# Two output tiles of chunk 14 multiplied while its y are made, the other four one behind the other, chunk 15's products in a new order

## What is computed

```
hs  = groupnorm(x)                        # per pixel 768 channels, 4096 pixels an image
xs  = silu(depthwise_conv3x3(hs @ in_proj.T) + conv_b)      # 1536 channels
dt, B, C = split(xs @ x_proj.T)           # 48, 4 and 4 columns
delta = softplus(dt @ dt_w + dt_b)
h[t] = exp(delta*A) * h[t-1] + (delta*xs)*B       # a scan over the pixels, 4 states a channel
y   = sum_n h[t,n]*C[t,n] + D*xs
y   = layernorm over the 1536 channels
x   = x + y @ out_proj.T                  # 768 channels
```

## Time and profile before

| | |
|---|---|
| time, median of 3 runs | 3519.16 us (3517.67 to 3519.83) |
| the profiled execution's own time | 3515.45 us |
| its span, first to last instruction | 3513.4 us |
| TensorE busy / VectorE / ScalarE / GpSimd | 3303.4 / 2848.3 / 2436.5 / 2366.1 us |
| mean granted TensorE clock | 0.980 |
| layer 0's last addition to x, end | 2601.5 us |
| layer 1's first instructions | 2604.0 us |

### The profile page before, as it was taken

The page is one execution under the profiler, slowest core; times in us unless marked ns, Lnnn a source line. Parts: engine busy times, 40 slices in busy tenths (PEclk is TensorE's granted clock), DMA queues, the critical chain, the costliest instruction groups (busy, mean ns, idle before and its releaser), DMA issues. The chain is left out here.

```text
span 3513.4 us, 38815 instructions
## 1 busy us (share of the span) xinstructions
PE 3303.4 (94%) x10616; PEld 1690.2 (48%) x10616; DVE 2848.3 (81%) x4084; ACT 2436.5 (69%) x4194; POOL 2366.1 (67%) x1566
## 2 busy tenths in 40 slices
PE   5967999999999999999999999997989999999998
PEld 2422343434334343443433434342347877777887
DVE  7799999999999999999999999998733355565532
ACT  3688888888888888888888888886535565433211
POOL 3399999999999999999999999999800001022111
PEclk9987999999999999999999999998999999999999
DMA  9444555565555655555565555646442233366654
GB/s 381 152 106 98 142 150 145 149 168 140 155 143 151 165 148 152 145 150 155 141 168 139 160 140 152 168 119 186 108 117 69 63 99 107 121 212 212 213 185 157
DMA packets 213736, 529.89 MB, mean 151 GB/s; under 512 B 25144, under 2 KB 46328, under 8 KB 208272
## 3 DMA queue, kind: packets, MB, share of 16 engines
q1 hardware_dynamic: 170512, 376.39, 33.4%
q0 software_dynamic: 43008, 151.02, 20.0%
HBM read 346.17 MB, written 80.48 MB: 121 GB/s over the span
## 5 line engine op out<-in xcount | busy, mean ns | idle before, releaser
L554 PE MATMUL p_in<-xn,win_v 128*128 128x512 f32 (+1 forms) x2160 | 976.7, 600 | 50.6 <-ACT halo L825 30.5
L570 PE MATMUL p_op<-uy,wout_ring 128*128 128x512 f32 x2160 | 975.5, 601 | 23.6 <-DVE x_res L1083 23.5
L1018 POOL TENSOR_TENSOR g_ring<-du,bc 128x2048 f32<-128x2048 f32 x192 | 870.8, 4535 | 15.1
L1046 DVE TENSOR_TENSOR_SCAN p_da<-p_da,state,g_ring 128x512 f32<-128x512 f32 x672 | 827.4, 1277 | 42.4 <-issue 28.7
L1069 DVE SCALAR_TENSOR_TENSOR p_cv<-win_v,conv_w,p_cv 128x512 f32<-128x512 f32 x960 | 723.1, 753 | 47.5 <-ACT p_cv L883 26.5
L554 PEld LDWEIGHTS p_in<-xn,win_v 128*128 128x128 f32 x2160 | 402.9, 192 | 594.1 <-issue 592.4
L570 PEld LDWEIGHTS p_op<-uy,wout_ring 128*128 128x128 f32 x2160 | 404.8, 191 | 581.5 <-issue 543.5
L764 ACT ACTIVATE p_da<-delta,A 128x512 f32<-128x512 f32 x768 | 500.0, 683 | 12.8 <-ACT state L769 0.4
L1052 DVE TENSOR_TENSOR g_ring<-p_da,bc 128x512 f32<-128x512 f32 x768 | 487.6, 677 | 0.0
L1524 PE MATMUL banks<-x_split,w_split 128*128 128x512 f32 x1152 | 458.1, 398 | 12.6 <-DVE x_split L1727 6.7
L1526 PE MATMUL banks<-x_split,w_split 128*128 128x512 f32 x1152 | 450.0, 391 | 0.0
(11 more groups left out here) (250 smaller groups left out, 4176.1 us busy)
## 6 DMA issues: line engine op xcount, KB each, us to landing
g_ring<-g_ring POOLq DMA_DIRECT2D x192, 512.0 KB, 5.2
win_v<-in_win SPq DMA_DIRECT2D x192, 384.0 KB, 3.1
wout_ring<-wout_scratch SPq DMA_DIRECT2D x184, 384.0 KB, 4.1
x_ring<-x_scratch SPq DMA_DIRECT2D x192, 256.0 KB, 2.7
q_scratch<-q_ring POOLq DMA_DIRECT2D x96, 256.0 KB, 2.5
x_split<-q_scratch SPq DMA_DIRECT2D x96, 256.0 KB, 3.4
out<-x_ring POOLq DMA_DIRECT2D x96, 256.0 KB, 2.9
x_res<-in_x SPq DMA_DIRECT2D x90, 256.0 KB, 4.6
```

The costliest lines, as they stand in the source:

```text
L554: last = nc.tensor.matmul(bank_in(i)[:, 0:n], WR[:, i % NW, t, :], XN[:, t, off:off + n], start=(t == 0), stop=(t == XT - 1))
L570: last = nc.tensor.matmul(p_op[:], OR[:, e % NO, k - h * HALF, :], ucol(c * K + k), start=(k == 0), stop=(k == K - 1))
L1018: nc.gpsimd.tensor_tensor(G[:, i % NG], DU[:].unsqueeze(1).broadcast_to([P, NS, N]), BB[:], ALU.mult).then_inc(s_dbu, 1)
L1046: nc.vector.tensor_tensor_scan(bank, bank, G[:, i % NG, n, :], init, ALU.mult, ALU.add)\
```

## The change

`early_products` multiplies chunk 14's output tiles m = 0 and 1 into p_in and p_cv, four k at a time (EARLY_E: slots 193, 195, 198 for m = 0; 194, 196, 200 for m = 1), with WOA, which is loaded two slots earlier than before (192). `out_proj_e` makes tiles 2 and 3 in p_op, 4 in p_in and 5 in p_cv, through the ring, in slots 199 to 203. VectorE scales and adds the six in the order 2, 0, 1, 3, 4, 5, one a slot in 201 to 206, into x tiles that SP loads to places in UY in slot 199, beside chunk 15's six. The number of products, additions, squares and stores is the same. `last_products` now makes all six tiles of chunk 15, by the table LAST, in slots 204 to 212.

```diff
@@ -237,9 +237,21 @@
...
         CL = NCH - 1
-        S_PAIR = K * CL + L_SQ
+        CE = CL - 1
+        S_E = S_OP + K * CE
+        HE = 2 * XT * CE
+        OE = XT * CE
+        ORDER_E = (2, 0, 1, 3, 4, 5)
+        EARLY_E = {S_E - 6: (0, 0, 4), S_E - 5: (1, 0, 4), S_E - 4: (0, 4, 8), S_E - 3: (1, 4, 8), S_E - 1: (0, 8, 12),
+                   S_E + 1: (1, 8, 12)}
+        LAST = {S_E + 5: (((2, 3), 0, 6),), S_E + 6: (((4,), 0, 7),), S_E + 7: (((0,), 0, 8),), S_E + 8: (((1,), 0, 9),),
+                S_E + 9: (((2, 3), 6, 9), ((4,), 7, 9)),
+                S_E + 10: (((0,), 8, 11), ((1,), 9, 11), ((2, 3), 9, 11), ((4,), 9, 11)),
+                S_E + 11: (((0,), 11, 12), ((1,), 11, 12), ((2, 3), 11, 12), ((4,), 11, 12)),
+                S_E + 12: (((5,), 0, 3),), S_E + 13: (((5,), 3, 12),)}
...
+        s_woa, s_ope, s_xle = sem("q_woa"), sem("q_ope"), sem("q_xle")
@@ -396,11 +419,11 @@
...
                 def load_wout(e):
-                    if e < 2 * XT * CL + 4:
+                    if e < HE + 12:
...
                         m, h = divmod(e % (2 * XT), 2)
-                        if e >= 2 * XT * CL:
-                            m += XT - 2
+                        if e >= HE:
+                            m += 2 if e < HE + 8 else 0
@@ -482,25 +505,31 @@
...
                                          .partition_broadcast(P)).then_inc(s_c[h], 16)
+                    if S == NT:
+                        sp.wait_ge(s_inp, NT)
+                        for m in range(2):
+                            sp.dma_start(WOA[:, m], woc_d[m]).then_inc(s_woa, 16)
                     if S == NT + 2:
-                        sp.wait_ge(s_inp, NT)
...
                         sp.wait_ge(s_ct, 2 * NT)
-                        for m in range(4):
-                            dst = WOA[:, m] if m < 2 else WOB[:, m - 2]
-                            sp.dma_start(dst, woc_d[m]).then_inc(s_wol, 16)
-                    if S == S_PAIR:
-                        sp.wait_ge(s_op, 2 * XT * (CL - 1))
+                        for m in range(2):
+                            sp.dma_start(WOB[:, m], woc_d[2 + m]).then_inc(s_wol, 16)
+                    n, m = out_e(S, 2)
+                    if n is not None:
+                        sp.wait_ge(s_ov, OE + n + 1)
+                        sp.dma_start(x1_d[B - 1, :, m, T - 2 * N:T - N], x_e(m)).then_inc(s_xsl, 16)
+                    if S == S_E:
+                        sp.wait_ge(s_op, HE)
+                        for m in range(XT):
+                            sp.dma_start(x_e(m), XTR[B - 1, :, m, T - 2 * N:T - N]).then_inc(s_xle, 16)
...
                             sp.dma_start(last_x(m), XTR[B - 1, :, m, T - N:T]).then_inc(s_xll, 16)
-                for e in range(SLOTS - S_OP + 1, 2 * XT * CL + 4):
-                    load_wout(e)
...
                 for n in range(NX):
-                    sp.wait_ge(s_xrs[n], 16 * ((XT * CL - n + NX - 1) // NX))
-                sp.wait_ge(s_xsl, 32 + 16 * XT)
+                    sp.wait_ge(s_xrs[n], 16 * ((OE - n + NX - 1) // NX))
+                sp.wait_ge(s_xsl, 32 + 32 * XT)
...
             def _(pe):
@@ -572,34 +601,63 @@
...
-                def last_products(ms, ks):
+                def early_products(m, ks):
...
                     if ks[0] == 0:
-                        pe.wait_ge(s_wol, WST + 16 * 4)
-                        if ms[0] == 0:
+                        pe.wait_ge(s_woa, 32)
+                        if m == 0:
...
                             pe.wait_ge(s_hout, houts(NT - 1))
+                        else:
                             pe.wait_ge(s_tap, len(TAPS) * NT)
-                        else:
+                    pe.wait_ge(s_y, K * CE + ks[-1] + 1)
+                    for k in ks:
+                        last = nc.tensor.matmul(bank_e(m), WOA[:, m, k, :], ucol(K * CE + k),
+                                                start=(k == 0), stop=(k == K - 1))
+                    if ks[-1] == K - 1:
+                        last.then_inc(s_ope, 1)
...
+                def out_proj_e(m, h):
...
+                    e = HE + 2 * (m - 2) + h
+                    if h == 0:
+                        pe.wait_ge(s_ov, OE + m - 2)
+                    pe.wait_ge(s_wor[e % NO], 16 * (e // NO + 1))
+                    for k in range(h * HALF, (h + 1) * HALF):
+                        last = nc.tensor.matmul(bank_e(m), OR[:, e % NO, k - h * HALF, :], ucol(K * CE + k),
+                                                start=(k == 0), stop=(k == K - 1))
+                    last.then_inc(s_op, 1)
...
+                def last_products(ms, ks):
...
+                    if ks[0] == 0:
+                        if ms[0] < 2:
+                            pe.wait_ge(s_ov, OE + 5 + ms[0])
+                        elif ms[0] == 2:
+                            pe.wait_ge(s_wol, WST + 16 * 2)
...
                             pe.wait_ge(s_rstd, CL)
+                        elif ms[0] == 4:
+                            pe.wait_ge(s_ov, OE + 4)
+                        else:
+                            pe.wait_ge(s_ls, NCH)
...
                     for k in ks:
                         for m in ms:
-                            w = WOA[:, m] if m < 2 else WOB[:, m - 2]
-                            last = nc.tensor.matmul(last_bank(m), w[:, k, :], ucol(K * CL + k),
+                            if m < 4:
+                                w = WOA[:, m, k, :] if m < 2 else WOB[:, m - 2, k, :]
+                            else:
+                                h = k // HALF
+                                e = HE + 2 * m + h
+                                if k % HALF == 0:
+                                    pe.wait_ge(s_wor[e % NO], 16 * (e // NO + 1))
+                                w = OR[:, e % NO, k - h * HALF, :]
+                            last = nc.tensor.matmul(last_bank(m), w, ucol(K * CL + k),
                                                     start=(k == 0), stop=(k == K - 1))
-                            if k == K - 1:
+                            if m < 4 and k == K - 1:
...
-                def last_out_proj(m):
-                    for h in range(2):
-                        e = 2 * XT * CL + 2 * (m - 4) + h
-                        pe.wait_ge(s_wor[e % NO], 16 * (e // NO + 1))
-                        for k in range(h * HALF, (h + 1) * HALF):
-                            last = nc.tensor.matmul(last_bank(m), OR[:, e % NO, k - h * HALF, :], ucol(K * CL + k),
-                                                    start=(k == 0), stop=(k == K - 1))
-                        last.then_inc(s_op, 1)
+                            if m >= 4 and k % HALF == HALF - 1:
+                                last.then_inc(s_op, 1)
@@ -659,11 +717,6 @@
...
                               .then_inc(s_ln, 1)
-                    if S_PAIR < S < S_PAIR + K and (S - S_PAIR) % 2:
-                        last_products((0, 1), range(S - S_PAIR - 1, S - S_PAIR + 1))
-                    if S >= S_PAIR + 6 and S < S_PAIR + 12:
-                        k = 2 * (S - S_PAIR - 6)
-                        last_products((2, 3), range(k, k + 2))
@@ -673,6 +726,14 @@
...
                         out_proj(c, m, range(h * HALF + 3, (h + 1) * HALF))
+                    if S in EARLY_E:
+                        m, k0, k1 = EARLY_E[S]
+                        early_products(m, range(k0, k1))
+                    if S_E <= S < S_E + 2:
+                        out_proj_e(2, S - S_E)
+                    if S_E + 2 <= S < S_E + 5:
+                        out_proj_e(S - S_E + 1, 0)
+                        out_proj_e(S - S_E + 1, 1)
@@ -691,6 +752,8 @@
...
                         last.then_inc(s_rsb, 1)
+                    for ms, k0, k1 in LAST.get(S, ()):
+                        last_products(ms, range(k0, k1))
@@ -701,9 +764,6 @@
...
                         first_row(new + 1)
-                pe.wait_ge(s_ov, XT * CL)
-                last_out_proj(4)
-                last_out_proj(5)
...
             def _(act):
@@ -1084,6 +1151,21 @@
...
+                def scale_e(n, m):
+                    if m < 2:
+                        vec.wait_ge(s_ope, m + 1)
+                    else:
+                        vec.wait_ge(s_op, HE + 2 * (m - 2) + 2)
+                    vec.wait_ge(s_rstd, CL)
+                    nc.vector.tensor_tensor(bank_e(m), bank_e(m), RS[:], ALU.mult).then_inc(s_oa, 1)
...
+                def add_e(n, m):
+                    o = m * CPB + CPB - 2
+                    vec.wait_ge(s_oa, OE + n + 1)
+                    vec.wait_ge(s_xle, 16 * XT)
+                    nc.vector.scalar_tensor_tensor(x_e(m), bank_e(m), bm[:, m:m + 1], x_e(m), ALU.add, ALU.add,
+                                                   accum_out=sum1[:, B - 1, o:o + 1]).then_inc(s_ov, 1)
...
                 def statistics(n, qs):
@@ -1136,6 +1218,10 @@
...
                         residual_add(r)
+                    n, m = out_e(S, 0)
```

(3 more changed lines are left out.)

28 lines of the change are left out of this document (21 added, 7 removed).

## The result

The changed kernel takes 3492.72 us (median of 5, 3490.03 to 3494.79) where the kernel before takes 3519.83: a ratio of 0.9925, with a 95% interval of 0.9912 to 0.9938, or 27.1 us less. Measured again in a later session it took 3493.21 us (0.9921, 0.9907 to 0.9936). The prediction was 3494.2 us, in a range of 3490 to 3504; it counted from 3519.16 us, the median of the first three of the five runs before.

A forecast was written before the change was run, and what follows sets the result against it. It took TensorE's own work, with waits before it, to bound layer 0's end. Gains of 27.0 and 23.3 gave a middle of 25.2, less 0.2 for stores: 25.0 off 3519.16 made 3494.2 us, range 3490 to 3504.

The forecast's parts named there:

- The 33.3 us of holes: TensorE time lost between 2399 and its last product: 25.8 us of waits and 7.5 of slow matmuls.
- The walk from slot to slot: TensorE's work and waits summed from slot 193 to 212: last product at 2573.0, a gain of 27.0 us.
- the list of holes: 33.3 us lost before, less 8.5 of remaining waits and 1.5 for the clock: a gain of 23.3 us.
- Slots 193 and 194: Blocks of 3.4 us before the last two x_proj products make the second x_dbl copy about 2.0 us late.
- The chain is now 1.7 late: At slot 200, RS of chunk 14 comes near 2467.4 against 2465.71, delaying decay, scan and softplus 1.7 us.
- The last y: Second bound, VectorE's chain: 2553.1 + 1.7 + 0.8 - 2.9 puts chunk 15's last y at 2552.7.
- 2 to 4 us: At the end, the path behind the last y finishes at 2571.1, this much before TensorE's own end.
- 1 to 13 us: Slots 204 to 212: each group of products finds its y, bank and weights ready this long before.
- The scan chain as the bound: Rival, chance 0.20: delayed scans decide the end; all delays give a gain of 16.5, 3502.6 us; cases between, 3497 to 3505.
- its three delays: Possible delays to the scans: 3.3 us (x_proj), 3.4 (slot 197's pair behind its block), 7.3 (x loads).
- Nothing gained: Rival, chance 0.03: all six blocks (20.6 us) and the loads pass into the scans; gain 2.7, 3516.5 us.
- slower by the clock: Rival, chance 0.04 including something unseen: granted clock falls in the dense stretch, 2449 to 2574; up to 3556 us.

The follow-up runs named there:

- pe_plus5: Changed kernel plus five unneeded products (ten matmuls) on TensorE in slot 206, ahead of tile 0's; layer 1 began 4.30 us later.
- tail_late: Changed kernel with chunk 15's tile 4 put back behind the norm's spreading, beside tile 5; 6.64 us later in the trace, 3496.41 us in all.
- no_early: Changed kernel without 16 of its 24 early products (k 0 to 7 of tiles 0 and 1, slots 193 to 196); 0.05 us later.
- split: Changed kernel with two y of chunk 14's tile 5 between slot 203's delta pairs and slot 208's products ahead of its sums; 196.48 us against 194.76.
- y_plus7: Changed kernel with additional VectorE multiplications between scans, eight in slot 207 and six in slot 208; end 15.0 us later.
- hole193: Changed kernel with slot 193's early block enlarged and ahead of the half tile, slot 194's behind x_proj, others smaller; 0.80 us earlier.
- best: Changed kernel with early blocks in the longest waits, two y between slot 203's delta pairs, slot 208's products ahead of its sums; 3486.21 us, ratio 0.9905.
- y_plus2: Changed kernel with five additional VectorE multiplications between the scans of slot 207; end 8.9 us later.
- late_block: Changed kernel with the last early block (tile 1, y 8 to 11) moved from slot 200 to slot 201; 5.92 us later.

## Why the prediction was right, and where it was not

In the changed kernel's trace all is 0.89 us later than in that of before because its mark is; the figures below have this taken off.

- **The mechanism** held: TensorE's own work behind the holes is the bound, the holes take other work in for little, and the tail is level with VectorE's additions (from 2566.40 on they follow each other without a wait, the last product ends at 2573.39 and the last addition starts at 2573.43). pe_plus5 (4.3 us more work, 4.3 later), tail_late and no_early (13.8 us less in the holes, the same end) show it. VectorE's timeline has the last addition's first half:

```profile
2573.43 0.70 DVE L1256 TENSOR_TENSOR p_ln<-p_ln,ln_rstd 128x512 f32<-128x512 f32 x1
```

- **The 33.3 us of holes.** The walk from slot to slot gave a last product at 2573.0, the list of holes 3.7 later; I took "the middle", 2574.8. It came at 2572.5. The walk was right to 0.5 us, in part by luck: it had the spreading of slot 200 at 2466.4, where 2464.5 came, 1.9 too late, and tile 5 of chunk 14 at 2494.7, where 2493.6 came, so that the stretches behind were taken 1.4 too short in all. (Its last line names five sums and spreadings; its total holds with six, and the trace has six.) The step that failed is the averaging: two sums that don't meet are no reason for their mean. Both charged a slow half tile in slot 199, which this execution did not have (5.42), and the list had waits of 8.5 in all where 6.8 came. Layer 1 began at 2576.6, not "near 2579": a gain of 27.45 in the trace and 27.1 in the medians, where 25.0 was summed. With slot 199's half tile at 7.1, as in split and y_plus7, the trace's gain would have been about 25.8: that it lies above the sum is in good part the clock of this execution.
- **Slots 193 and 194.** The second copy of x_dbl was forecast "near 2408.3" and came at 2408.45; TensorE's waits of "0.8 and 0.9" were 0.72 and 0.79. Slot 198's sums waited 0.26, not 1.5, for the square; slot 199 2.29, not 2.7; in slot 201 RS and the addition cost 0.78 + 0.56 for a forecast of 1.0, tile 4 waited nothing for p_in, where 0.3 was forecast, and the second delta pair of slot 203 waited 1.40 for 1.3.
- **"The chain is now 1.7 late"** at RS is a second step that fell: 2467.4 was forecast, 2465.58 came, 0.1 earlier than before. The delay was there up to slot 199 (1.4 us at its half tile) and was paid back by that half tile at the full clock, 1.56 us. hole193 and best show that it is real: without it slot 199's half tile starts 2.3 us sooner, and where that half tile is at the full clock (best) so does the pair.
- **The last y** came at 2551.2 in place of 2552.7: the 1.7 didn't reach it. "2 to 4 us" of spare against TensorE's end: 3.1 at the last sums (the last square ends at 2552.74, the sums start near 2555.8), 3.0 at slot 209's products. The tightest place is slot 208's sums with 0.9. The prediction had no figure for it: its "1 to 13 us" are for groups of products, and its spare is counted at the end alone.
- **The scan chain as the bound (0.20):** it needed delays of several us in the scans; 0.9 would already have begun to show. The first of its three delays came in part: the second copy of x_dbl was 2.1 us late, the scans that start from 2454.5 to 2463.8 still 1.4, the one at 2474.5 no longer. The second did not: ScalarE waited 0.15 us for slot 197's pair. Of the third little came: GpSimd's accumulating transfers took 6.7 us in the median in place of 5.6, and two additions of GpSimd waited 0.92 and 1.21, at no cost to the end that shows. What the loads alone cost was not tried by a run of its own.
- **Nothing gained, or slower by the clock:** 1.00 granted from 2470 to 2575, in the changed kernel and in best (2465 to 2570). So the dense stretch did not lose the clock. Slow matmuls were seen behind waits: 1.7 us (no_early), 3.0 (y_plus2, behind a wait that the edit put into the dense stretch) and 5.0 (late_block).

## What to carry to other kernels

Cut the timeline at an event that doesn't move (here the pair behind RS) and count work and waits on either side: work moved from the dense side into a wait on the other side is gained, less what it still delays there (1.7 us of one block's 3.4, 2.3 us for the blocks of slots 193 and 194). Slow matmuls behind waits can hide such a delay or be taken for one. When a chain must be given time, put ready work ahead of the instruction that waits for it; look for the spare of every consumer in queue order, and not of the last alone. Compare such small changes between two fixed events inside a trace, and look for slow matmuls behind waits before a difference of 1 to 5 us is put down to an edit.
